# Eight of the nine additions of finished count tiles issued by GpSimd instead of VectorE

## The reference, cut to what matters

```python
h = relu(layernorm(x) @ W1 + b1) @ W2 + b2              # W1 512x256, W2 256x512
x = x + h + segment_sum(h[dst], src, 1250)              # row, col = src, dst
y = layernorm(x)
g = softmax(y @ W_gate + b_gate) - 0.25 * sigmoid(y @ W_thr + b_thr)
w = where(g >= 0, g, 0); w = w / sum(w)
x = x + sum over 8 experts of w[e] * (y @ W_exp[e] + b_exp[e])
```

## Time and profile before

| | us |
|---|---|
| median of three runs | 397.3 |
| the profiled execution, whole | 397.86 |
| span in its profile, first to last instruction | 396.1 |
| TensorE busy | 372.4 |
| VectorE busy | 287.3 |
| ScalarE busy | 105.2 |
| GpSimd busy | 6.1 |

### The profile page before, as it was taken

The page is one execution under the profiler, slowest core; times in us unless marked ns, Lnnn a source line. Parts: engine busy times, 40 slices in busy tenths (PEclk is TensorE's granted clock), DMA queues, the critical chain, the costliest instruction groups (busy, mean ns, idle before and its releaser), DMA issues.

```text
span 396.1 us, 5931 instructions
## 1 busy us (share of the span) xinstructions
PE 372.4 (94%) x1890; PEld 242.7 (61%) x1890; DVE 287.3 (73%) x440; ACT 105.2 (27%) x189; POOL 6.1 (2%) x33
## 2 busy tenths in 40 slices
PE   0999999898999989989999999999999999999996
PEld 0877787565555653556666666666666666666663
DVE  3799987999889839882696665855757657567653
ACT  4734354454676303554201001010010100100000
POOL 6000000000000000000000000000000000000000
PEclk9999999999999998996999999999999999999999
DMA  8700011552532215310020030110300300000133
GB/s 177 180 2 13 16 38 40 135 152 91 161 98 81 83 32 117 137 61 0 2 76 31 0 106 2 53 54 0 106 0 0 105 0 0 0 0 0 60 97 103
DMA packets 16808, 23.87 MB, mean 60 GB/s; under 512 B 2796, under 2 KB 9683, under 8 KB 16660
## 3 DMA queue, kind: packets, MB, share of 16 engines
q1 hardware_dynamic: 16382, 23.05, 19.9%
q10 hardware_dynamic: 403, 0.53, 0.6%
HBM read 14.77 MB, written 2.56 MB: 44 GB/s over the span
## 4 chain that ended last, share of the span: by engine, by line
PE 82%; DVE 8%; DMA 4%; issue 3%; DVEq 1%; ACT 1%; SPq 0%; ACTq 0%
PE ps_g L978 17%; PE ps_g L979 17%; PE ps_g L980 17%; PE ps_g L866 10%; PE ps_w L904 8%; PE ps_g L942 4%; DMA late<-counts 3%; DVE split L636 3%; PE ps_g L852 2%; DVE stats L601 2%; DMA dst_i<-in_dst_dram 1%; PE ps_w L896 1%; PE ps_w L942 1%; PE ps_a L952 1%; PE ps_g L854 1%
## 5 line engine op out<-in xcount | busy, mean ns | idle before, releaser
L978 PE MATMUL ps_g<-we_hi,split 128*125 128x512 f16 x320 | 122.4, 383 | 0.4 <-DVE x_sb L762 0.4
L979 PE MATMUL ps_g<-we_lo,split 128*125 128x512 f16 x320 | 122.2, 382 | 0.0
L980 PE MATMUL ps_g<-we_hi,split 128*125 128x512 f16 x320 | 122.0, 381 | 0.0
L762 DVE SCALAR_TENSOR_TENSOR x_sb<-ps_g,weight_s,x_sb 125x512 f32<-125x512 f32 x80 | 60.0, 750 | 56.2 <-PE ps_g L980 56.1
L636 DVE TENSOR_TENSOR split<-places,keys 125x1536 f16<-125x1536 int16 (+2 forms) x125 | 91.4, 796 | 8.9 <-PE ps_w L904 5.2
L767 DVE SCALAR_TENSOR_TENSOR x_sb<-late,weight,x_sb 125x512 f32<-125x512 f32 x80 | 60.0, 751 | 9.6 <-DVE x_sb L762 5.5
L978 PEld LDWEIGHTS ps_g<-we_hi,split 128*125 128x125 f16 x320 | 44.1, 138 | 26.3 <-DVE x_sb L762 0.8
L980 PEld LDWEIGHTS ps_g<-we_hi,split 128*125 128x125 f16 x320 | 44.1, 138 | 25.8 <-issue 0.8
L979 PEld LDWEIGHTS ps_g<-we_lo,split 128*125 128x125 f16 x320 | 44.1, 138 | 25.4 <-issue 0.6
L904 PE MATMUL ps_w<-split 125*128 125x250 f16 x402 | 53.0, 270 | 3.3 <-issue 1.6
L866 PE MATMUL ps_g<-late,r_sb 125*128 125x512 f32 (+3 forms) x120 | 51.4, 533 | 3.8 <-DMA late<-counts 3.7
(11 more groups left out here) (129 smaller groups left out, 194.3 us busy)
## 6 DMA issues: line engine op xcount, KB each, us to landing
stage<-in_L_ffn_W_exp_dram SPq DMA_DIRECT2D x8, 1024.0 KB, 5.3
late<-counts SPq DMA_DIRECT2D x50, 122.1 KB
x_sb<-in_x_dram SPq DMA_DIRECT2D x5, 448.0 KB, 11.4
out_dram<-x_sb SPq DMA_DIRECT2D x10, 224.0 KB
late<-in_L_ffn_b_exp_dram SPq DMA_DIRECT2D x1, 2000.0 KB
w_sb<-in_L_gnn_W_dram SPq DMA_DIRECT2D x2, 512.0 KB, 6.6
x_sb<-in_x_dram ACTq DMA_DIRECT2D x1, 260.0 KB
out_dram<-x_sb ACTq DMA_DIRECT2D x10, 26.0 KB
```

Of the source, the lines that this page charges most:

```text
L762: nc.vector.scalar_tensor_tensor(out=x_sb[:, i, :], in0=ps_exp[(TILES * par + i) % RING], scalar=weight_s[:, ds(e, 1), i], in1=x_sb[:, i, ...
L978: nc.tensor.matmul(bank, xhi[:, k, tokens[i]], hi_w, start=(k == 0), stop=False)
L979: nc.tensor.matmul(bank, xhi[:, k, tokens[i]], lo_w, start=False, stop=False)
L980: mm = nc.tensor.matmul(bank, xlo[:, k, tokens[i]], hi_w, start=False, stop=(k == KD - 1))
```

## The change

Additions 1 to 8 are taken out of VectorE's loop and written at the end of GpSimd's program, in the same order, with the same waits and the same semaphore. Addition 9 stays on VectorE, at its place, and now waits for addition 8 of the other engine. The waits of the SP queue are unchanged.

```diff
@@ at the end of GpSimd's program
+            for i in range(1, TILES - 1):
+                moved(pool, i)
+                if i > 1:
+                    pool.wait_ge(a_summed, i - 1)
+                nc.gpsimd.tensor_tensor(a_sum, a_t[0] if i == 1 else a_sum, a_t[i % 3], ALU.add).then_inc(a_summed, 1)
@@ VectorE's program
-            def column_sum(i):
-
-                moved(dve, i)
-                if i > 1:
-                    dve.wait_ge(a_summed, i - 1)
-                nc.vector.tensor_tensor(a_sum, a_t[0] if i == 1 else a_sum, a_t[i % 3], ALU.add).then_inc(a_summed, 1)
-
             for w in range(NW):
                 compare(w)
                 if w in NORM_AT:
                     first_norm(NORM_AT[w])
-                if w >= 3 * WPT + 1 and (w - 1) % WPT == 0:
-                    column_sum((w - 1) // WPT - 2)
-            column_sum(TILES - 2)
...
             low_weights(0, 0)
-            column_sum(TILES - 1)
+            moved(dve, TILES - 1)
+            dve.wait_ge(a_summed, TILES - 2)
+            nc.vector.tensor_tensor(a_sum, a_sum, a_t[(TILES - 1) % 3], ALU.add).then_inc(a_summed, 1)
```

## The result

The kernel after the change takes 401.8 us (median of four runs, 399.5 to 403.0) against 397.2 before: a ratio of 1.011, with a 95% interval of 1.008 to 1.015. The profiled execution took 401.5 us with a span of 399.7, 3.6 us more than before. The time landed where the forecast put it. Most of the loss has another cause.

A forecast was written before the change was run, and what follows sets the result against it. TensorE was taken as the bound, VectorE as runner-up. Removal was worth 0; VectorE's setbacks of 7.91 us, less 1.73 of waits and 2.15 of lead, made 4.0: 397.3 + 4.0 = 401.3 us, range 396.9 to 405.5.

The forecast's parts named there:

- the mechanism I had given 0.07: Rival: late addition 1 on GpSimd holds block 15's move in the SP queue and the 1 MB load behind; 400.4 us, chance 0.07.
- the 4.0 us of the sum: TensorE's predicted delay by block 47, from comparisons held up by GpSimd additions, carried to the end.
- What bounds the kernel: Claim that TensorE sets the pace from 65 to 139.6 us, VectorE is runner-up, and relieving VectorE brings 0.
- G: Length of one addition on GpSimd, taken as 2.5 us, between 1.25 and 3.75.
- All of G falls on VectorE: Claim that each GpSimd addition holds up VectorE's two-input comparisons for its full length, 2.5 us; lower bound nothing.
- The sum: By block 47: seven setbacks, 7.91 us, less 1.73 of removed waits, less 2.15 of lead: TensorE 4.0 us late.
- the setback of VectorE: VectorE's loss per addition 1 to 7: the GpSimd addition's length minus 1.37 us freed, 1.13 us.
- rule of lead and setback: TensorE's delay is VectorE's added setbacks, less removed waits, beyond its lead over TensorE: 1.6 us at block 37, 2.15 at 47.
- It adds while VectorE compares: Step claiming GpSimd's additions run beside VectorE's comparisons, as tiles are ready about when VectorE adds them today.
- The rival's price: For a first addition of 8 us: SP queue stands 3.1 us, TensorE late by up to as much, 400.4 us; chance 0.07.
- VectorE's lead: How far comparisons end before TensorE begins the block: 1.6 us at block 37, 2.15 at block 47.

The follow-up runs named there:

- e4: The changed kernel without additions 1 to 8 on either engine and without the SP queue's waits for them; addition 9 adds tile 9 to itself: 397.1 us, ratio 0.999.
- e9: The kernel before, plus eight GpSimd additions of 125x1250 on a buffer of their own, one per landed tile, nobody waiting for them: 404.2 us, ratio 1.021.
- e10: The kernel before, plus eight GpSimd `iota` instructions that only write a 125x1250 buffer of their own, one per landed tile: 395.1 us, ratio 0.995.
- e2: The changed kernel with addition 1 back on VectorE behind block 16, additions 2 to 8 still on GpSimd: 396.8 us, ratio 0.998.
- e8: The kernel with only addition 1 back on VectorE, plus a second same-size GpSimd addition behind each of its seven, on its own buffer: 415.1 us, ratio 1.039.
- e12: The changed kernel with a ring of four tiles instead of three, so block 20 and not 15 first waits for addition 1: 397.5 us, ratio 1.001.
- e5: The changed kernel with a small VectorE memset behind the comparisons of blocks 15, 16 and 17: 397.6 us, ratio 1.004.
- e1: The changed kernel with one small GpSimd addition (128x8) in front of the eight, as a first use beforehand: 403.4 us, ratio 1.015.
- e11: The kernel with only addition 1 back on VectorE, with the second layer's weights and bias loaded after block 31 instead of 8: 399.9 us, ratio 1.006.

## Why the prediction was right, and where not

Number and sign were right: 401.3 us forecast, 401.8 measured. The closeness is luck: most of the loss came by the mechanism I had given 0.07, and the 4.0 us of the sum did not come by theirs.

- **What bounds the kernel: right.** VectorE set no pace; e4, without eight additions, is 0.999 of before.
- **G: nearly right.** Taken as 2.5 us. The shortest additions take 2.40 us. What matters is how long a comparison is held: `wg` at L668 takes 2.39 us beside addition 8 instead of 0.19, so 2.2 us:

```profile
141.20 2.39 DVE L668 SCALAR_TENSOR_TENSOR wg<-wg_sb,wg 128x36 f16<-128x36 f32 x1
```

The estimate from the Trainium skill's page "GPSIMD Engine Reference", section 3.1, 2.75 us, is above both.
- **All of G falls on VectorE: right for the comparison that comes second**, as that line, e9 and e10 show. The rule of "SBUF — State Buffer", section "Who interferes with whom", agrees with the trace in who collides: readers do, a writer does not. In who waits it tells half. The comparison that comes second waits for one addition; the addition that comes second waited for nine comparisons, not for one, and for over thirty in e9.
- **The sum: the term that failed is the 4.0 us of TensorE's delay from comparisons.** Matmuls waited 0.7 us for comparisons, in e4 without additions 0.9. With 2.2 us per addition the setback of VectorE is 0.83 instead of 1.13 us, and my own arithmetic gives 7 x 0.83 - 1.73 - 2.15 = 1.9 us by block 47 instead of 4.0, and for e2, with six, 1.1. The traces neither confirm nor exclude that much. From its start at tile 3 to its start at tile 9 TensorE takes 47.4 us before and 48.3 in e2 (95.56 to 143.86), but also 48.4 in e10 (94.95 to 143.30), where no comparison is held up; and the ratio of e2 leaves at most 0.5 us. That collisions reach TensorE when additions come close together is shown (e8, e9); that the rule of lead and setback has the right size is not.
- **"It adds while VectorE compares": the step that hid the cause.** I let addition 1 have 4.9 us, saw that 8 us would be too many, and gave that little chance, because I took the sharing for a queue in which each gets its turn. It took 8.6, and the load behind block 15's move was issued 2.9 us late. The rival's price, up to 3.1 us, counted the late queue and left out the clock: 1.7 us of later start and 3.1 us of slow stretch came. The wait of the SP queue for addition 1 was the sign named for it.
- **Range and chances.** 396.9 to 405.5 holds the result; slower had 0.66. Without the rival at 0.07 the change would have been about even, as e2 shows, so the right number came from a term too large and a rival too small.

## What to carry to other kernels

An operation moved off a full engine must be asked two things: does it still need what the full engine holds, and who waits for it. Here the relief was worth nothing since the engine was not the bound, the collision of GpSimd's reads with two-input VectorE instructions stayed under VectorE's lead, with a cost too small to tell from the spread, and a single waiter with some 2 us of slack, a DMA queue with a large load behind it, made the loss. A side job with a deadline needs a buffer more (e12), or stays where it is (e2); a gap in VectorE's stream helped in one trace (e5).

## What the runs showed of the hardware

- Comparisons of VectorE that follow each other without a gap can keep a GpSimd addition that reads SBUF out for long: nine passed beside addition 1 of the changed kernel, thirteen in e1, over thirty VectorE instructions in e9. They start so close together that each begins about 0.08 us before its forerunner's recorded end. Every addition that was kept out for four or more of them got in where that overlap was smaller or gone; in the changed kernel it was 0.05 us, since the first two comparisons shown here end at 81.76 + 1.42 = 83.18 and the next, which is the one held up, begins at 83.13:

```profile
81.76 1.42 DVE L642 TENSOR_TENSOR split<-places,keys 125x1152 f16<-125x1152 int16 x2
83.13 5.79 DVE L642 TENSOR_TENSOR split<-places,keys 125x1152 f16<-125x1152 int16 x2
```

That is not the whole condition: additions 3, 6 and 8 of the changed kernel got in at the next VectorE instruction although it overlapped its forerunner by 0.08 us. What decides stays open. While kept out, the addition's recorded duration grows: some 2.4 us of work showed as 8.6, 11.3 and 27.1 us.
- TensorE's granted clock was 0.50 from 97.2 to 104 us (1.2 GHz in place of 2.4); it fell within a wait of 2.89 us. In e2, with a wait of 0.74 us at that place, it stayed at 1.00, and in e11 also around one of 2.15 us. So a start at tile 3 that was 1.7 us later had cost 4.8 us by tile 4.
